# The order of each engine's queue: by the longest chain of work behind a stretch instead of by which is ready first

## What is computed

```python
x = x + _L0_attn_a_ref(_layernorm(x), ...)   # mamba
x = x + _L0_ffn_ref(_layernorm(x), ...)      # experts: a gate and 8 networks 128 -> 512 -> 128, selu
x = x + _L0_attn_b_ref(_layernorm(x), ...)   # linear attention, with a norm of its own
x = x + _L0_ffn_ref(_layernorm(x), ...)
x = x + _L1_attn_a_ref(_layernorm(x), ...)   # 16 heads of 64, window 64, convolutions
x = x + _L1_ffn_ref(_layernorm(x), ...)      # channel mix
x = x + _L1_attn_b_ref(_layernorm(x), ...)   # delta rule
x = x + _L1_ffn_ref(_layernorm(x), ...)
x = x + _L2_attn_a_ref(_layernorm(x), ...)   # state space, all batches together
x = x + _L2_ffn_ref(_layernorm(x), ...)      # low rank linear
x = x + _L2_attn_b_ref(_layernorm(x), ...)   # mixed precision attention
x = x + _L2_ffn_ref(_layernorm(x), ...)
x = x + _L3_attn_a_ref(_layernorm(x), ...)   # causal attention, 16 heads of 8
x = x + _L3_ffn_ref(_layernorm(x), ...)      # deep network 128 -> 512 -> 512 -> 512 -> 128
x = x + _L3_attn_b_ref(_layernorm(x), ...)   # causal attention, 16 heads of 8
x = x + _L3_ffn_ref(_layernorm(x), ...)
```

## Time and profile before

| | |
|---|---|
| median of 3 runs | 3379.39 us (3374.99 to 3385.18) |
| the profiled execution | 3381.56 us, its span 3380.3 us |
| busy share of the span | PE 81%, PEld 54%, DVE 65%, ACT 40%, POOL 24% |
| instructions | 40884 |
| HBM traffic | 52.32 MB read, 1.44 MB written |
| mean granted clock of TensorE | 0.88 of full speed |

### The profile page before, as it was taken

How to read it: one execution, slowest core, us unless ns; L and a number is a source line. 1 busy time by engine, 2 the same in 40 slices (tenths; PEclk the granted TensorE clock), 3 DMA queues, 4 the chain that set the end, 5 groups by cost and what they waited for, 6 DMA issues and landing times. The chain is left out here.

```text
span 3380.3 us, 40884 instructions
## 1 busy us (share of the span) xinstructions
PE 2748.1 (81%) x15606; PEld 1823.3 (54%) x15606; DVE 2180.7 (65%) x4187; ACT 1345.9 (40%) x2289; POOL 796.7 (24%) x628
## 2 busy tenths in 40 slices
PE   5689798886557766898978987977978989869888
PEld 1247575554257522566755655846955555445454
DVE  7988786777989679888877768554055242462331
ACT  5423234663343354333456645322023333324242
POOL 3830001214794037300012117301010000110100
PEclk8899897998779688999989978968989999889899
DMA  3000001110000000000021120002800000000000
GB/s 140 0 1 1 1 1 25 35 30 15 0 1 1 31 0 0 1 1 1 3 83 35 29 63 1 1 0 68 275 1 1 1 1 1 7 1 1 1 1 7
DMA packets 51924, 73.16 MB, mean 22 GB/s; under 512 B 5777, under 2 KB 41361, under 8 KB 51089
## 3 DMA queue, kind: packets, MB, share of 16 engines
q1 hardware_dynamic: 51728, 70.56, 6.8%
HBM read 52.32 MB, written 1.44 MB: 16 GB/s over the span
## 5 line engine op out<-in xcount | busy, mean ns | idle before, releaser
L132 POOL TENSOR_SCALAR shifted<-moments 128x4 f32<-128x4 f32 x68 | 19.5, 287 | 1615.1 <-DVE moments L156 1615.1
L108 PEld LDWEIGHTS ps<-held_ffn,hidden 128*128 128x128 f32 x2304 | 300.6, 193 | 167.0 <-issue 106.8
L121 ACT ACTIVATE grown<-ps,bias_grown 128x512 f32<-128x512 f32 x288 | 197.9, 687 | 346.4 <-PE ps L108 333.7
L108 PE MATMUL ps<-held_ffn,hidden 128*128 128x128 f32 x2304 | 311.4, 279 | 28.6 <-DVE hidden L135 27.8
L135 DVE SCALAR_TENSOR_TENSOR conv<-conv_in,held_l1a,conv 128x512 f32<-128x512 f32 x288 | 224.5, 789 | 71.2 <-ACT conv L121 67.1
L129 POOL TENSOR_TENSOR part<-state,c_rows 128x512 f32<-128x512 f32 x128 | 231.5, 1831 | 82.0 <-PE ps L108 38.8
L129 POOL TENSOR_TENSOR long<-long,product 128x512 f32<-128x512 f32 x136 | 210.2, 1565 | 56.3 <-ACT product L121 46.9
L135 DVE SCALAR_TENSOR_TENSOR hidden<-ps,bias_kept,grown 128x512 f32<-128x512 f32 x288 | 211.4, 744 | 4.2
L129 POOL TENSOR_TENSOR qk<-conv,held_const 128x512 f32<-128x512 f32 x64 | 98.6, 1541 | 436.4 <-DVE conv L135 436.4
L132 DVE TENSOR_SCALAR grown<-grown,bias_fallen 128x512 f32<-128x512 f32 x288 | 140.5, 489 | 94.1 <-ACT grown L121 92.8
L108 PE MATMUL ps<-yn,nT 128*128 128x192 f32 (+1 forms) x640 | 120.0, 338 | 61.3 <-DVE yn L129 43.4
(11 more groups left out here) (438 smaller groups left out, 6166.7 us busy)
## 6 DMA issues: line engine op xcount, KB each, us to landing
ring<-lags SPq DMA_DIRECT2D x64, 512.0 KB, 4.6
turned<-conv SPq DMA_DIRECT2D x256, 64.0 KB, 2.0
held_ffn<-in_ffn SPq DMA_DIRECT2D x1, 4690.0 KB, 18.9
held_l1a<-in_l1a SPq DMA_DIRECT2D x2, 2120.0 KB, 15.9
held_l3f<-in_l3f SPq DMA_DIRECT2D x1, 2824.0 KB, 11.1
held_rows<-in_rows SPq DMA_DIRECT2D x1, 1044.5 KB, 8.3
out<-x SPq DMA_DIRECT2D x4, 256.0 KB, 2.6
held_const<-in_const SPq DMA_DIRECT2D x1, 785.0 KB, 4.8
```

What stands on the lines that cost most here:

```text
L108: return self.sent(self.real.matmul(out, lhsT, rhs, **kw), cost, 0.15)
L121: return self.sent(self.real.activation(out, a, func, **kw), cost)
L132: return self.vector(self.real.tensor_scalar(out, a, p, q, *ops), columns(out))
```

## The change

Nothing is added to or taken from the computation. `run` is now gone through twice. The first time (`weigh`) no instruction is issued: each engine is replaced by an object that ignores every call, the old rule is used, and for each stretch the planner notes which stretches wait for it. Backwards over that list every stretch gets a `tail`: its own planned cost and the largest tail among those that wait for it or follow it in its lane. The second time the same set of candidates is looked at (those that could start soonest on the engine; `patience` is 0), and of them the one with the largest tail is taken, with 20 us (`AHEAD`) added for stream A. BEHIND still comes last.

```diff
+AHEAD = 20.0
@@ def advance(self, lane):
+        stretch = Stretch()
         if lane.asked is not None:
             signal, n = lane.asked
-            at = signal.when(n)
-            e.free = max(e.free, at)
-            if e.known.get(signal.sem.num, 0) < signal.base + n:
+            e.free = max(e.free, signal.when(n))
+            if self.trial:
+                signal.raisers[n - 1].then.append(stretch)
+            elif e.known.get(signal.sem.num, 0) < signal.base + n:
...
+        if self.trial:
+            if lane.stretches:
+                lane.stretches[-1].then.append(stretch)
+            lane.stretches.append(stretch)
+            self.order.append(stretch)
@@ def run(self):
             for e in self.engines.values():
-                for lane in e.lanes:
-                    if lane.over:
-                        continue
-                    ready = 0.0 if lane.asked is None else lane.asked[0].when(lane.asked[1])
-                    if ready is None:
-                        continue
-                    key = (max(ready, e.free), lane.rank == BEHIND, ready, lane.rank)
-                    if best is None or key < best[0]:
-                        best = key, lane
+                open_ = [(start, lane) for lane in e.lanes if not lane.over
+                         and (start := self.start_of(lane)) is not None]
+                if not open_:
+                    continue
+                soon = min(start for start, _ in open_) + self.patience
+                start, lane = min(((start, lane) for start, lane in open_ if start <= soon), key=self.choice)
+                if best is None or start < best[0]:
+                    best = start, lane
...
+    patience = 0.0
+
+    def choice(self, option):
+        start, lane = option
+        ready = 0.0 if lane.asked is None else lane.asked[0].when(lane.asked[1])
+        if self.trial or self.rule == 0:
+            return lane.rank == BEHIND, ready, lane.rank
+        tail = lane.stretches[lane.at].tail if lane.at < len(lane.stretches) else 0.0
+        return lane.rank == BEHIND, -tail - (lane.rank == 1) * AHEAD
+
+    rule = 1
+
+    def weigh(self):
+        real = {e: e.real for e in self.engines.values()}
+        self.trial = True
+        for e in real:
+            e.real = Quiet()
+        end = self.run()
+        for stretch in reversed(self.order):
+            stretch.tail = stretch.cost + max((q.tail for q in stretch.then), default=0.0)
...
@@ def build(m):
+    m.weave.weigh()
     m.weave.run()
```

More of the change, by code:

```diff
@@ L95, in sent @@
         e = self.engine
+        self.weave.spent += cost
         e.free += cost
@@ L107, in matmul @@
             cost = max(cost, 0.225 if slow else 0.06)
-        return self.sent(self.real.matmul(out, lhsT, rhs, **kw), cost, 0.15)
+        return self.sent(self.engine.real.matmul(out, lhsT, rhs, **kw), cost, 0.15)
     def transpose(self, out, a, ident):
-        return self.sent(self.real.transpose(out, a, ident), 0.112, 0.15)
+        return self.sent(self.engine.real.transpose(out, a, ident), 0.112, 0.15)
     def activation(self, out, a, func, **kw):
@@ L119, in activation @@
             if table is EXP_AND_LN:
-                self.real.preload_act_table_set(EXP_AND_LN)
-        return self.sent(self.real.activation(out, a, func, **kw), cost)
+                self.engine.real.preload_act_table_set(EXP_AND_LN)
+        return self.sent(self.engine.real.activation(out, a, func, **kw), cost)
     def vector(self, ins, n):
@@ L163, in dma_start @@
         n = columns(out) * out.shape[0] * 4
-        return Sent(self, self.real.dma_start(out, a), self.engine.free + 2.2 + n / 180e3)
+        return Sent(self, self.engine.real.dma_start(out, a), self.engine.free + 2.2 + n / 180e3)
 BEHIND = 9
+AHEAD = 20.0
 class Weave:
@@ L179, in __init__ @@
         self.made = 0
+        self.trial = False
+        self.spent = 0.0
+        self.order = []
+        self.seen = []
     def raised(self, lane, signal, ins, by, at):
         engine = lane.engine
+        if self.trial:
+            if not signal.times:
+                self.seen.append(signal)
+            signal.times += [at] * by
+            signal.raisers += [lane.stretches[-1]] * by
+            return
         if signal.sem is None:
@@ L220, in advance, with start_of @@
             lane.over = True
+        stretch.cost = self.spent
+        lane.at += 1
+    def start_of(self, lane):
+        ready = 0.0 if lane.asked is None else lane.asked[0].when(lane.asked[1])
+        return None if ready is None else max(ready, lane.engine.free)
     def run(self):
@@ L241, in run, with __init__ @@
         return max(e.free for e in self.engines.values())
+    patience = 0.0
+    def choice(self, option):
+        start, lane = option
+        ready = 0.0 if lane.asked is None else lane.asked[0].when(lane.asked[1])
+        if self.trial or self.rule == 0:
[11 more added lines that the diff above has]
+            stretch.tail = stretch.cost + max((q.tail for q in stretch.then), default=0.0)
+        for signal in self.seen:
+            signal.reset()
+        for e in real:
+            e.real, e.free, e.table = real[e], 0.0, None
+            for lane in e.lanes:
+                lane.reset()
+        self.trial = False
+        return end
+class Stretch:
+    def __init__(self):
+        self.cost, self.tail, self.then = 0.0, 0.0, []
 class Stream:
```

39 lines of the change are left out of this document (25 added, 14 removed).

## The result

The change makes the kernel slower: 3508.81 us, the median of four runs (3502.32 to 3519.01), against 3382.28 in the four runs of before beside them, a ratio of 1.036 (95% interval 1.032 to 1.039). The forecast was 3348 us, with a range of 3305 to 3400. The profiled execution of the change took 3514.17 us around a span of 3512.8.

The account below looks back on a forecast made before the run. No engine fills the span (PE busy 81%, DVE 65%); the full engine changes by layer, and reordering only fills gaps. 14 + 12 + 11 - 6 = 31 us less gives 3348 us against the 3379.39 median, range 3305 to 3400.

Parts of the forecast that it names:

- cannot make any instruction shorter: Whole kernel: a reordering only fills gaps, where one stream's chain waits or the two streams ask for different engines.
- Distance in the first pair: First pair of layers: stream A ahead early, 17 to 63 DVE instructions at the experts; 14 us less, bounds 0 and 25.
- the making of the filter: First pair's delta rule, 352 us against 299 in the second: 53 us longer, carries the filter, and that stays.
- measured example: Second pair, already about 70 DVE instructions apart, taken to show a larger distance's worth: 1108 us against 1186, 78 less.
- Second pair: Second pair and barrier before state space: nothing gained, distances 47 to 70 for 43 to 79.
- this test itself: Second pair: a change by over 15 us either way makes the prediction wrong; fine order then counts more than distance.
- Deep network beside attention: Second list: attention's step stands between smaller matmul pieces, three meetings at 4 us each; 12 us less, bounds 0 and 63.
- the end: Last 66 us, A alone with 14.1 us of PE idle: some 3 us idle would stay; 11 us less.
- Function sets: ACT: 11 more set loads, 10 in the second list, 1.28 us each; half of those 10 counted, 6 us more.
- the sign named: State space to the end: PE busy over 84% would show the forecast's steps right.
- The first rival: In and behind mamba: plan out of step with the chip, wrong turns 0.8 us each; slower, 3392 us, chance 26%.
- The third rival: Whole kernel: much more gain, 79 us less, 3300 us; denser PE would raise low granted clocks; chance 14%.

## Why the prediction was wrong

The step under all others that failed is the sentence that a reordering "cannot make any instruction shorter" and can only fill gaps. PE's busy time was thus taken as fixed, but the same 15606 matmuls took 105 us more of it, at a mean granted clock of 0.855 in place of 0.880. Part by part:

- **Distance in the first pair (14 less): the number came out for stream A alone, and the step beside it failed.** Mamba and experts took 314 us for 326, 12 less, and A reached the first windowed attention 17 us earlier. B reached it 4 us later (521.5 became 525.8). A left that layer 18 us earlier and B 24 later, so the two together had gained nothing by then; the forecast counted A's starts only. B's first transposes there came 37 us behind A's (forecast 25 to 35). The failed step is the sentence that the making of the filter "stays": the 53 us by which the first delta rule is longer than the second were taken as the filter's fixed price. They are a price at a distance of 18 us. At 52 us it is 74 more, and nearly the same distance without the filter costs 12. How the filter does it is shown in part: four of its 4.4 us instructions hold up steps of A's recurrence, and in pieces it costs less; 32 of the 81 us are lost ahead of the recurrences and stay open. The second pair, taken as the "measured example" of a larger distance, has no filter, and could not show this.
- **Second pair (nothing): wrong, by 91 us.** The text named this test itself: over 15 us there, and the fine order inside the layers counts for more than the distance. It does. 67 of the 91 are the windowed attention, and the kernel with the rule in that layer alone loses 59 us in all. Of the 67, 45 are PE at a lower clock, for which the sum had no term.
- **Deep network beside attention (12 less) and the end (11 less): of the right kind and size.** The second list takes 890 us for 902. The last 66 us have 4.8 us of idle PE for 14.1, 9 less; the rest of the list gains 3 with the set loads in it. 78 set loads of 1.28 us came as forecast, and no wait for ACT in the last layers is over 0.8 us. PE is busy 86% from state space to the end (the sign named was 84%), but it was 85% before, so this sign could not tell.
- **Function sets (6 more):** not measured apart. The 3 us that the rest of the list gains would be the forecast's 12 less with 9 of loads taken off, or a smaller gain and hidden loads. By the 2.66 us a switch of the Trainium skill, page "ScalarE: Activation LUTs", section "What ACT_TABLE_LOAD costs", ten loads would be 27 us, an estimate. The trace has 1.283 us for each of the 78, and in the median the next activation starts 1.3 us after the load did, so it shows no drain.
- **The first rival** had the right sign and named the second pair as its sign, with 26%. Its place (mamba) and its price (0.8 us a wrong turn, 3392 us) were not what happened: its sum had no term for the clock, and the waits that count are those of 4.8 us at which both streams stand. The third rival spoke of the clock, in the other direction. In the profile of before, PE's 37 idle us in the second windowed attention looked like a reserve. The clock was 0.91 with them, and none of the longest-chain orders in that layer has kept it there (0.72 to 0.84).

## What to carry to other kernels

Two copies of one loop on shared engines did best here about a third (or two thirds) of a period apart and worst at the same step. A rule that holds them a fixed amount of work apart should be checked against the work of one turn of the loop, here 19.0 us for a handicap of 20; it locked them in one of the two pairs. Work that fills gaps did better in short pieces (up to 3 us in place of 8), which was worth more here (31 us in the kernel before, 96 in the change, one execution each) than any order. When two streams are cut by the starts of one of them, look at the other too: a gain of one can be a loss of the other. And an idle engine's gaps are not all alike: before spending them, see what clock stands beside them.

## What the runs showed of the hardware

- Within a standstill of PE of 4.80 us the granted clock fell to the lower of its two levels and stayed there until 1931, over 10 us of work; by an estimate from the 32 matmuls in those 12 us against 26 to 29 in 6, the wait cost about twice its own length. In the same layer the clock fell as often behind a single idle piece of 1.3 to 1.5 us, while in the kernel before it stayed at the upper level for 88 us with 10 us of idle time in pieces of up to 1.22. A lower clock without more idle time was seen too (0.76 with 38 us idle, 0.91 with 37). What the chip answers to stays open.
- The granted clock differed between executions of the same order: 0.83 to 0.90 in one layer, 286 to 303 us.
- DVE's products of 128x4096 float32 took 7.0 to 8.2 us when they square the filter's power or its start (18.5 once in each of two executions), and 4.4 when they multiply back and ahead; the sums took 4.4. It is the operands that go with the difference and not POOL's work, as the expectation on the pieces has it: with POOL idle the squarings still took 7.1 to 7.2 us (the filter put off, from 1372 us on).
